# Even and odd features instead of lower and upper halves: a stationary tile of TensorE that takes every second fp32 of a row

## The chip, the core and the metric

The kernel runs on one core of one Trainium2 chip. The metric is device time in microseconds for one execution of the whole kernel, the median of three runs. TensorE, VectorE, ScalarE and the DMA queues of SyncE all work at the same time; the time is set by whichever chain of them ends last.

## What is computed

Two graph layers over 4096 nodes with 256 features, both with the same 4096 x 4096 adjacency matrix. Cut to what matters:

```python
# layer 0
deg = sum(adj, axis=1) + 1e-5
out = ((adj / deg) @ x) @ W_neigh.T + b_neigh + x @ W_self.T + b_self
x1  = layernorm(x + relu(out))
# layer 1
d   = where(rowsum > 0, rowsum ** -0.5, 0)
out = ((d[:, None] * adj * d[None, :]) @ x1) @ W + b
y   = layernorm(x1 + relu(out))
```

The work is in the two products with the adjacency matrix: 4096 x 4096 times 4096 x 256, in fp32.

## The kernel before

**Precision by three passes.** An fp32 number is split into a rounded part (hi) and a remainder (lo), both in the format fp32r, which TensorE takes in one pass. A product is then the sum of three matmuls: x_hi with a_hi, x_hi with a_lo, x_lo with a_hi (line 674). ScalarE makes hi by a copy (L256), VectorE makes lo by a subtraction (L389).

**Tiling of the main matmuls.** The nodes of the result come in 8 blocks of 512 (`NB`, `IB`). For one block the kernel runs over 16 units (`NU`) of two node tiles each (`UJ` = 2, a tile is 128 nodes). For each unit it takes both feature halves `f` and both tiles `q`, and does the three passes: 2 x 2 x 3 = 12 matmuls a unit at L675. In each of them the stationary operand is a 128 x 128 piece of x (128 nodes on the partitions, 128 features in a row), and the moving operand is 128 x 512 of the transposed adjacency matrix. The result, 128 features x 512 nodes, is summed in PSUM in `ps_main[parity][:, f, :]`. The stationary operand changes with every matmul, so each matmul has a weight load of its own (LDWEIGHTS, the rows marked PEld).

**Where the stationary operand lies.** In layer 0 it is read from `xs`, shaped [128, 32, 2, 256]: per partition and node tile, 256 fp32 of hi and then 256 fp32 of lo. In layer 1 it is read from `zs` (28 tiles) and `xs` (4 tiles) in the same layout. The function `stationary` (L154 to L159) gives the slice: 128 neighbouring fp32, from `f * P` on. The first two units of the first block are an exception (L657): they run before hi and lo exist, in plain fp32 straight from the loaded `x_stage(0)` and `raw`. A plain fp32 matmul is done as two passes, so the trace has 16 of them, and there are 24 fewer at L675.

**What surrounds them.** SyncE loads one unit of the adjacency matrix (512 KB) into a ring of four slots (`raw`). ScalarE makes `hi` of it, VectorE `lo`; in layer 0 VectorE also adds the unit into `acc` (L565) for the row sums. TensorE waits for `lo` (`l_ready`, L669), does its 12 matmuls and signals `unit_done`. Slots are freed by `unit_done` and `l_ready`. The order is written out by hand: between units of the main matmuls stand pieces of the previous block's epilogue and of the current block's prologue. Both use `product` (L608): six matmuls with a moving operand of 256 columns (L613), whose stationary operands are the feature-major results `st_hi` and `st_lo`, 128 nodes in a row. One of these groups follows each of the units 1 to 4 (epilogue) and, in layer 0, 9 to 12 (prologue, one unit later in the first block). In layer 0 there is also one group of eight loads and matmuls for the row sums at L634. The last block has an epilogue of its own (L693), after everything else.

**The order of features.** The partition `p` of `ps_main[:, f, :]` is a feature. The second product contracts over it, so the rows of the weight matrices (`contraction_rows`, L709) and of the transposed x (`xt`, L717) must be laid out in the same order of features. Both are arranged on the host, ahead of the kernel.

Of the kernel before, what the change touches and what calls it, by code (L numbers as in the profile page):

```python
# [24 lines left out]
F = 256  # L25
P = 128
FH = F // P
JT = N // P
IB = 512
NB = N // IB  # L30
# [13 lines left out]
def build(nc, x_nat, xt_in, adj_in, wn_in, bn_in, ws_in, bs_in, w1_in, b1_in, out):  # L44
# [6 lines left out]
    with ctx:  # L51
        def sb(name, shape, dt=f32):
            return ctx.enter_context(nc.sbuf_tensor(name, shape, dt))
# [6 lines left out]
        xs = sb("xs", [P, JT, 2, F], f32r)  # L60
# [7 lines left out]
        xt = sb("xt_sb", [P, FH, IB])  # L68
# [54 lines left out]
        def slot(u):  # L123
            return u % RING

        def is_last(e):

            return isinstance(e, int) and e == NB - 1
# [8 lines left out]
        def x_stage(c):  # L137

            if c == 0:
                return acc[:, 1, :].rearrange("p (t f) -> p t f", t=XC)  # L140
            return (res, tt)[c % 2][:, :, :]
# [12 lines left out]
        def stationary(layer, part, jt, f):  # L154

            if layer == 0:
                return xs[:, jt, part, f * P:(f + 1) * P]
            src = zs[:, jt] if jt < ZOWN else xs[:, jt - ZOWN]
            return src[:, part, f * P:(f + 1) * P]  # L159

        def layers(eng, one_block, last_epilogue):

# [444 lines left out]
        def _(pe):  # L607
# [9 lines left out]
            def prologue(b, u):  # L617

                t = u - xt_unit(b)
                if 0 <= t < TB:  # L620
                    if t == 0:
                        pe.wait_ge(wl_ready, 2)
                        pe.wait_ge(xtl_ready, b + 1)

                    product(ps_epi[:, t, F:2 * F], slice(t * P, (t + 1) * P), lambda part, k: ws[:, part, k, :])

            def epilogue(layer, e, parity, u):
                n = e + layer * NB
                if u == 0 and layer == 0:

                    pe.wait_ge(acc_folded, e + 1)
                    pe.wait_ge(ones_set, 1)
                    for t in range(TB):
                        last = pe.matmul(ps_epi[:, TB - 1, t:t + 1], acc[:, parity, t * P:(t + 1) * P],  # L634
                                         ones[:, :], start=True, stop=True)
                    last.then_inc(rs_summed, 1)
                if 1 <= u < 1 + TB:
                    t = u - 1
                    if t == 0:
                        pe.wait_ge(stl_ready, n + 1)  # L640
                    if t == TB - 1 and layer == 0:
                        pe.wait_ge(rs_copied, e + 1)

                    product(ps_epi[:, t, 0:F], slice(t * P, (t + 1) * P),
                            lambda part, k: moving_weight(layer, part, k)).then_inc(tile_done, 1)

            def one_block(layer, b, parity, epi):
                g0 = b * NU + layer * NB * NU
                ps = ps_main[parity]
                for u in range(NU):  # L650
                    if epi is None and u < WHOLE:

                        pe.wait_ge(x_first_full[u], 16)
                        pe.wait_ge(raw_full[slot(u)], 16)
                        for f, q in [(f, q) for f in range(FH) for q in range(UJ)]:
                            jt = u * UJ + q
                            last = pe.matmul(ps[:, f, :], x_stage(0)[:, jt, f * P:(f + 1) * P],  # L657
                                             raw[:, slot(u), q * IB:(q + 1) * IB], start=(jt == 0), stop=False)
                        last.then_inc(unit_done, 1)
                        continue  # L660
                    if epi is None and u % 2 == 0:
                        pe.wait_ge(xl_ready, u // 2 + 1)
                    if layer == 1 and epi[0] == 0:
                        pe.wait_ge(z_ready, UJ * (u + 1))
                    if layer == 1 and epi[0] == 1 and u == 0:
                        pe.wait_ge(wl_ready, 3)


                    pe.wait_ge(l_ready, g0 + (u + 1))  # L669
                    ends = layer == 1 and is_last(b) and u == NU - 1  # L670
                    for f, q in [(f, q) for f in range(FH) for q in range(UJ)]:
                        jt = u * UJ + q
                        cols = slice(q * IB, (q + 1) * IB)
                        for i, (part, mov) in enumerate(((0, hi), (0, lo), (1, hi))):
                            last = pe.matmul(ps[:, f, :], stationary(layer, part, jt, f), mov[:, slot(u), cols],  # L675
                                             start=(jt == 0 and i == 0), stop=(jt == JT - 1 and i == 2))
                        if ends and q == UJ - 1:
                            last.then_inc(half_done, 1)
                    if not ends:
                        last.then_inc(unit_done, 1)  # L680
                    if epi is not None:
                        epilogue(*epi, 1 - parity, u)
                    if layer == 0:
                        prologue(b, u)

            def last_epilogue(epi):
                n = 2 * NB - 1
                passes = [(st_hi, 0), (st_hi, 1), (st_lo, 0)]
                for k in range(FH):
                    pe.wait_ge(stl_ready, n + 1 + k)  # L690
                    for t in range(TB):
# [4 lines left out]
                        if k == FH - 1:  # L696
                            last.then_inc(tile_done, 1)

            layers(pe, one_block, last_epilogue)


# [33 lines left out]
```

## Time and profile before

| | us |
|---|---|
| median of three runs | 800.5 |
| lowest and highest | 799.44, 802.32 |
| span of the profiled execution | 800.8 |
| TensorE matmul busy | 782.1 (98%), 3704 instructions |
| TensorE weight load busy | 653.0 (82%), 3704 instructions |
| VectorE busy | 577.4 (72%) |
| ScalarE busy | 386.9 (48%) |

The profile is of one execution. Matmuls are pipelined: the duration of one (about 390 ns for 512 columns) is longer than the distance from its start to the next one's, so how many are done in a time is read from the starts or from long stretches, not from the duration. A weight load is shown on a lane of its own (PEld) and runs beside the matmul ahead of it. The waits of an engine say how long it stood and for whom; the chain that ended last says which stretches add up to the span.

### The profile page before, as it was taken

Reading aid. Unit: us, or ns where it says so; the run is one execution under the profiler, and the core shown is the slowest. Engines: PE = TensorE matmul, PEld = TensorE weight load, DVE = VectorE, ACT = ScalarE, POOL = GpSimd, SP = SyncE. Lnnn points to the kernel's source line nnn. Section 1 sums busy time; section 2 is a strip of 40 time slices with the busy share of each in tenths; the row PEclk is TensorE's granted clock in tenths of the full one; section 3 lists DMA queues with packets and bytes.
Section 4 is the critical chain, followed back from the end, with each engine's and each line's share of the span. In section 5 each row is a group of like instructions: output and inputs, shape, how many; then the busy total and the mean of one; then the engine's idle time right before and its main releaser. Section 6 shows DMA issues by size and latency. Waiting matters only on the chain.

```text
span 800.8 us, 11034 instructions
## 1 busy us (share of the span) xinstructions
PE 782.1 (98%) x3704; PEld 653.0 (82%) x3704; DVE 577.4 (72%) x868; ACT 386.9 (48%) x528; POOL 0.3 (0%) x6
## 2 busy tenths in 40 slices
PE   7899999999999999999999999999999999999995
PEld 4678888888888888888888888888888888888884
DVE  5799989899898998989966554555546455554643
ACT  3463745536446364454554545445444544545451
POOL 0000000000000000000000000000000000000000
PEclk9999999999999999999999999999999999999998
DMA  8767574755647556465565575746575574657540
GB/s 258 274 252 239 179 244 154 253 183 166 236 155 236 193 174 236 157 233 189 181 227 165 175 255 174 250 162 237 180 236 187 171 246 162 236 180 239 180 158 27
DMA packets 54459, 160.93 MB, mean 201 GB/s; under 512 B 5024, under 2 KB 18464, under 8 KB 54432
## 3 DMA queue, kind: packets, MB, share of 16 engines
q1 hardware_dynamic: 46224, 152.46, 56.6%
q10 hardware_dynamic: 8208, 8.13, 2.9%
q8 instruction: 15, 0.25, 0.1%
q14 instruction: 12, 0.10, 0.0%
HBM read 152.17 MB, written 8.39 MB: 201 GB/s over the span
## 4 chain that ended last, share of the span: by engine, by line
PE 94%; DMA 2%; DVE 2%; ACT 1%; issue 0%; SPq 0%
PE ps_main L675 84%; PE ps_epi L613 8%; DMA raw<-adj_t 2%; PE ps_main L657 1%; PE ps_epi L634 1%; DMA tt<-x_nat 1%; DVE lo L389 0%; DVE acc L565 0%; ACT hi L256 0%; PE ps_epi L693 0%; DVE tt L436 0%; DVE stats L585 0%; DVE tt L419 0%; DVE xs L389 0%; ACT tt L359 0%
## 5 line engine op out<-in xcount | busy, mean ns | idle before, releaser
L256 ACT ACTIVATE hi<-raw 128x1024 fp32r<-128x1024 f32 x254 | 269.4, 1061 | 352.8 <-PE ps_main L675 327.8
L389 DVE TENSOR_TENSOR lo<-raw,hi 128x1024 fp32r<-128x1024 f32 x254 | 310.4, 1222 | 145.3 <-ACT hi L256 145.2
L675 PE MATMUL ps_main<-hi,xs 128*128 128x512 f32 x1136 | 366.3, 392 | 4.3 <-DVE lo L389 4.3
L675 PE MATMUL ps_main<-hi,zs 128*128 128x512 f32 x896 | 283.0, 390 | 0.0
L675 PEld LDWEIGHTS ps_main<-hi,xs 128*128 128x128 f32 x1136 | 214.2, 189 | 49.3 <-DVE lo L389 3.6
L675 PE MATMUL ps_main<-lo,xs 128*128 128x512 f32 x568 | 222.4, 392 | 0.0
L675 PEld LDWEIGHTS ps_main<-hi,zs 128*128 128x128 f32 x896 | 168.3, 188 | 34.3
L675 PE MATMUL ps_main<-lo,zs 128*128 128x512 f32 x448 | 174.7, 390 | 0.0
L565 DVE TENSOR_TENSOR acc<-acc,raw 128x1024 f32<-128x1024 f32 x112 | 136.3, 1217 | 0.0
L675 PEld LDWEIGHTS ps_main<-lo,xs 128*128 128x128 f32 x568 | 107.3, 189 | 20.0 <-issue 0.2
L675 PEld LDWEIGHTS ps_main<-lo,zs 128*128 128x128 f32 x448 | 84.2, 188 | 16.3
L419 DVE SCALAR_TENSOR_TENSOR tt<-ps_epi,d_cur,bias 128x256 f32<-128x256 f32 x32 | 15.4, 483 | 39.2 <-PE ps_epi L613 38.5
L389 DVE TENSOR_TENSOR st_lo<-ps_main,st_hi 128x1024 fp32r<-128x1024 f32 (+1 forms) x17 | 19.8, 1162 | 21.6 <-ACT st_hi L256 21.6
L281 ACT ACTIVATE tt<-tt,nmr,inv_root 128x256 f32<-128x256 f32 x60 | 32.5, 588 | 4.3 <-DVE nmr L473 4.3
L256 ACT ACTIVATE st_hi<-ps_main 128x1024 fp32r<-128x1024 f32 (+1 forms) x17 | 16.6, 978 | 33.3 <-PE ps_main L675 33.3
L275 ACT ACTIVATE ps_epi<-tt,nmean 128x256 f32<-128x256 f32 x60 | 27.5, 459 | 0.0
L436 DVE SCALAR_TENSOR_TENSOR tt<-tt,res 128x256 f32<-128x256 f32 x64 | 26.8, 419 | 0.2
L613 PE MATMUL ps_epi<-ws_sb,st_hi 128*128 128x256 f32 x128 | 24.2, 282 | 0.0
L613 PE MATMUL ps_epi<-wn_sb,st_hi 128*128 128x256 f32 x128 | 24.2, 282 | 0.0
L613 PEld LDWEIGHTS ps_epi<-ws_sb,st_hi 128*128 128x128 f32 x128 | 22.0, 190 | 2.5
L613 PEld LDWEIGHTS ps_epi<-wn_sb,st_hi 128*128 128x128 f32 x128 | 22.0, 190 | 2.5
L613 PE MATMUL ps_epi<-xs,st_hi 128*128 128x256 f32 x112 | 21.2, 282 | 0.0
(74 smaller groups left out, 322.7 us busy)
## 6 DMA issues: line engine op xcount, KB each, us to landing
raw<-adj_t SPq DMA_DIRECT2D x256, 512.0 KB, 3.3
res<-x_nat SPq DMA_DIRECT2D x11, 512.0 KB, 6.4
xt_sb<-xt SPq DMA_DIRECT2D x8, 512.0 KB, 5.0
x_scratch<-tt ACTq DMA_DIRECT2D x8, 512.0 KB, 6.2
res<-x_scratch SPq DMA_DIRECT2D x8, 512.0 KB, 6.0
out<-tt ACTq DMA_DIRECT2D x7, 512.0 KB, 6.4
tt<-x_nat SPq DMA_DIRECT2D x4, 512.0 KB, 6.4
acc<-x_nat SPq DMA_DIRECT2D x2, 256.0 KB, 3.6
```

Of the source, the lines that this page charges most:

```text
L256: return act.activation(dst, src, ACT.Copy)
L275: act.activation(ps_epi[:, t, 0:F], tt[:, t, :], ACT.Square, bias=nmean[:, t:t + 1], accum_out=squares[:, t:t + 1]).then_inc(squares_ready, 1)
L281: act.activation(tt[:, t, :], tt[:, t, :], ACT.Identity, bias=nmr[:, t:t + 1], scale=rstd[:, t:t + 1]).then_inc(x1_ready, 1)
L389: return dve.tensor_tensor(dst, src, hi_part.bitcast(f32), ALU.subtract)
L419: ins = dve.scalar_tensor_tensor(out=tt[:, t, :], in0=ps_epi[:, t, 0:F], scalar=(rdeg, d_cur)[layer][:, t:t + 1], in1=(bias0, bias1)[layer ...
L436: link(dve.scalar_tensor_tensor(out=tt[:, t, :], in0=tt[:, t, :], scalar=0.0, in1=res[:, t, :], op0=ALU.max, op1=ALU.add, accum_out=sums[: ...
L565: dve.tensor_tensor(a, a, raw[:, slot(u), :], ALU.add).then_inc(acc_done, 1)
L613: last = pe.matmul(ps, st[:, k, rows], weight(part, k), start=(k == 0 and q == 0), stop=(k == FH - 1 and q == 2))
L634: last = pe.matmul(ps_epi[:, TB - 1, t:t + 1], acc[:, parity, t * P:(t + 1) * P], ones[:, :], start=True, stop=True)
L657: last = pe.matmul(ps[:, f, :], x_stage(0)[:, jt, f * P:(f + 1) * P], raw[:, slot(u), q * IB:(q + 1) * IB], start=(jt == 0), stop=False)
L675: last = pe.matmul(ps[:, f, :], stationary(layer, part, jt, f), mov[:, slot(u), cols], start=(jt == 0 and i == 0), stop=(jt == JT - 1 and ...
```

## The change

The two feature halves are no longer features 0 to 127 and 128 to 255, but the even and the odd ones. Half `f` takes `f:F:FH`, with `FH` = 2: 128 fp32 at a distance of 8 bytes, over 1020 bytes of the row, where before it took 128 neighbouring fp32, 512 bytes. Partition `p` of `ps_main[:, f, :]` is then feature `2p + f` instead of `f * 128 + p`, and the host lays out the rows of the weights and of the transposed x accordingly. The arrays have the same shapes and sizes as before, and their transfers are the same.

```diff
         def stationary(layer, part, jt, f):
             if layer == 0:
-                return xs[:, jt, part, f * P:(f + 1) * P]
+                return xs[:, jt, part, f:F:FH]
             src = zs[:, jt] if jt < ZOWN else xs[:, jt - ZOWN]
-            return src[:, part, f * P:(f + 1) * P]
+            return src[:, part, f:F:FH]
...
-                            last = pe.matmul(ps[:, f, :], x_stage(0)[:, jt, f * P:(f + 1) * P],
+                            last = pe.matmul(ps[:, f, :], x_stage(0)[:, jt, f:F:FH],
                                              raw[:, slot(u), q * IB:(q + 1) * IB], start=(jt == 0), stop=False)
...
     def contraction_rows(w):
-        return np.ascontiguousarray(w.reshape(FH, P, F).transpose(1, 0, 2))
+        return np.ascontiguousarray(w.reshape(P, FH, F))
...
-        "xt": np.ascontiguousarray(x.T.reshape(FH, P, NB, IB).transpose(2, 1, 0, 3)),
+        "xt": np.ascontiguousarray(x.T.reshape(P, FH, NB, IB).transpose(2, 0, 1, 3)),
```

No instruction is added, removed or moved on any engine. The loads for L613, L634 and L693 read what they read before, without a stride.

## Rows read from the trace of the kernel before

**Rows 1.** All cores: span in us and mean granted TensorE clock.
```profile
core 0: 800.8 us, clock 0.995
```

**Rows 2.** Page: busy time and instructions; shares of the chain that ended last.
```profile
PE 782.1 (98%) x3704; PEld 653.0 (82%) x3704; DVE 577.4 (72%) x868; ACT 386.9 (48%) x528; POOL 0.3 (0%) x6
...
PE 94%; DMA 2%; DVE 2%; ACT 1%; issue 0%; SPq 0%
```

**Rows 3.** Waits on TensorE: who for whom, us in total, times, longest.
```profile
PE ps_main L657 <- DMA raw<-adj_t: 5.4, 1, 5.4
PE ps_main L675 <- DVE lo L389: 4.3, 3, 3.1
```

**Rows 4.** Chain that ended last, in order of time: start us, us, what.
```profile
131.02 13.63 PE ps_main L675 x60
144.65 0.71 PE ps_epi L613 x6
145.36 2.75 PE ps_main L675 x12
...
166.65 0.79 PE ps_epi L634 x8
...
433.38 35.39 PE ps_main L675 x156
468.77 0.71 PE ps_epi L613 x6
```

**Rows 5.** TensorE's groups by form: line, engine, operation, count | busy us, mean ns | idle.
```profile
L675 PE MATMUL ps_main<-hi,xs 128*128 128x512 f32 x1136 | 366.3, 392 | 4.3 <-DVE lo L389 4.3
L675 PE MATMUL ps_main<-hi,zs 128*128 128x512 f32 x896 | 283.0, 390 | 0.0
L675 PE MATMUL ps_main<-lo,xs 128*128 128x512 f32 x568 | 222.4, 392 | 0.0
L675 PE MATMUL ps_main<-lo,zs 128*128 128x512 f32 x448 | 174.7, 390 | 0.0
...
L675 PEld LDWEIGHTS ps_main<-hi,zs 128*128 128x128 f32 x896 | 168.3, 188 | 34.3
```

**Rows 6.** Timeline, 432 to 434 us, TensorE and its loads: start us, us, what.
```profile
432.28 0.39 PE L675 MATMUL ps_main<-hi,zs 128*128 128x512 f32 x1
432.28 0.41 PEld L613 LDWEIGHTS ps_epi<-wn_sb,st_hi 128*128 128x128 f32 x2
432.51 0.40 PE L613 MATMUL ps_epi<-wn_sb,st_hi 128*128 128x256 f32 x2
432.63 0.19 PEld L613 LDWEIGHTS ps_epi<-wn_sb,st_lo 128*128 128x128 f32 x1
432.74 0.28 PE L613 MATMUL ps_epi<-wn_sb,st_lo 128*128 128x256 f32 x1
...
433.10 0.28 PE L613 MATMUL ps_epi<-wn_sb,st_lo 128*128 128x256 f32 x1
433.10 0.19 PEld L675 LDWEIGHTS ps_main<-hi,zs 128*128 128x128 f32 x1
433.22 0.40 PE L675 MATMUL ps_main<-hi,zs 128*128 128x512 f32 x1
433.22 0.19 PEld L675 LDWEIGHTS ps_main<-lo,zs 128*128 128x128 f32 x1
433.45 0.40 PE L675 MATMUL ps_main<-lo,zs 128*128 128x512 f32 x1
```

**Rows 7.** Timeline, 64 to 72 us, loads alone: the eight loads of L634.
```profile
65.48 1.08 PEld L634 LDWEIGHTS ps_epi<-ones,acc 128*128 128x128 f32 x8
```

**Rows 8.** Timeline, 23 to 33 us, where the granted clock was at half.
```profile
28.96 1.05 PE L675 MATMUL ps_main<-hi,xs 128*128 128x512 f32 x2
29.39 0.33 PEld L675 LDWEIGHTS ps_main<-lo,xs 128*128 128x128 f32 x1
29.82 0.63 PE L675 MATMUL ps_main<-lo,xs 128*128 128x512 f32 x1
```

**Rows 9.** Groups of VectorE from 131 to 381 us: busy us, mean ns | idle.
```profile
L389 DVE TENSOR_TENSOR lo<-raw,hi 128x1024 fp32r<-128x1024 f32 x80 | 97.7, 1221 | 19.5 <-ACT hi L256 19.5
```

**Rows 10.** Groups of all engines from 23.5 to 26.5 us, where TensorE stood.
```profile
L389 DVE TENSOR_TENSOR lo<-raw,hi 128x1024 fp32r<-128x1024 f32 x1 | 1.2, 1224 | 6.2 <-ACT hi L256 6.2
```

**Rows 11.** Busy us by stretch, one in each layer: PE, PEld, DVE, ACT.
```profile
200.00:300.00 100.00, 100.00 (x494) 84.72 (x493) 91.68 (x136) 51.19 (x72) 0.00 (x0) 1.00 0.59 199
600.00:700.00 100.00, 100.00 (x465) 83.63 (x464) 53.36 (x81) 47.95 (x64) 0.00 (x0) 1.00 0.61 202
```

## The prediction, made before the changed kernel had run

> **What bounds the kernel now.** I read the span and the granted clock first: one core, 800.8 us, clock 0.995 [rows 1], so nothing is to be explained by the clock but a short stretch near the start. Then the page: the matmul lane is busy 98% of the span, and 94% of the chain that ended last is TensorE [rows 2]. A busy matmul lane proves little, since matmuls overlap, so I looked at the waits: TensorE stood 5.4 us for the first adjacency tile and 4.3 us, in three pieces, for `lo` [rows 3], and for nothing else. From there to the last epilogue the reader is to see an unbroken row of matmuls whose distance sets the time.
>
> That distance comes from the chain in order of time: 60 matmuls of L675 took 13.63 us in layer 0, 227.2 ns each; 156 took 35.39 us in layer 1, 226.9 ns each [rows 4]. The counts by form add up to 1136 + 896 + 568 + 448 = 3048 matmuls at L675 [rows 5]; at 227 ns these are 692 us of the 800.8. The six matmuls of a `product`, 256 columns each, took 0.71 us, 118 ns each [rows 4]. By the counts of the page there are 3704 - 3048 = 656 others: 16 at L657, 64 at L634 (8 groups of 8), 24 at L693, and so 552 at L613, 92 groups of 6.
>
> So one nanosecond more between two main matmuls costs 3.0 us, 0.4% of the kernel. The question of this change is whether a weight load that reads every second fp32 makes that distance longer.
>
> **What the change does, part by part.** It adds, removes and moves no instruction. The transfers of weights and `xt` have the same sizes and land in the same places; the order of features is undone by the host's layout of the contraction rows. Splits, sums and norms read and write whole rows as before. All of this costs nothing, on the path or off it. What is left is the 3048 loads at L675 and the 16 at L657.
>
> First term, **the cover of a load**. The timeline shows when a load starts: the one for the matmul at 433.45 us starts at 433.22, with the matmul ahead of it [rows 6]. It therefore has the whole distance, 227 ns, before its own matmul is due. Its duration in the profile is 188 to 190 ns [rows 5], but that is from start to end with the way through the engine; the time for which it keeps the next one from starting is shorter. In a `product` a load starts at 432.63, its matmul at 432.74, 0.11 us later and before the load's record ends at 432.82 [rows 6]. Loads and matmuls follow each other there every 118 ns. The tightest test of the load alone is L634, whose moving operand is one column: eight loads in 1.08 us, the last one 0.19 long, so (1.08 - 0.19) / 7 = 127 ns from one to the next [rows 7]. So a load of 128 neighbouring fp32 takes its port for 118 ns at most beside fp32r matmuls, and 127 ns at most at L634. Of the 227 ns, 100 to 109 are free. A strided load costs nothing inside a unit as long as it takes less than 227 ns, 1.8 to 1.9 times as long as now.
>
> Second term, **how long a strided load takes**. No row shows one, so I bound it. Low end: it delivers as many numbers, one after the other, and takes what it takes now. An end below that would need the load to be held up by its neighbouring addresses, for which no row speaks; that is the fourth rival. High end: it reads at half the rate, since it covers 1020 bytes where it covered 512; that doubles 118 to 236, or 127 to 254 ns. The nearest row for how fast TensorE can go over addresses is its own moving operand: 512 fp32, 2048 bytes a partition, every 227 ns [rows 4], 9.0 bytes a ns. At that rate the 1020 bytes of a strided load, skipped ones included, take 113 ns, less than the 118 that are there already. That is read on another operand, so it is an analogy and not a proof, but it is the only row in which this engine's reads are seen at work, and it puts the strided load at its present length. I take zero for this term, and keep 0 and 254 - 227 = 27 ns times 3048 = 82 us as its ends.
>
> The Trainium skill (SBUF, Door 1: The DMA port swizzle, the remark on cachelines) says that an SBUF line has 16 bytes, that two hits on a line give full bandwidth, and that each crossing to a new line costs something. With 8 bytes between numbers there are two hits a line, which by the first half of the rule is free; but crossings double from one in four numbers to one in two, which by the second half speaks against the change. The sum would be 800.5 us by the first half and one of the slower rivals by the second.
>
> Third term, **loads with little cover**. A main load behind a matmul of 256 columns has 118 ns and not 227: the load at 433.10 belongs to the matmul at 433.22 [rows 6]. There are 92 of these, one behind each group of L613, and 8 more behind L634: 100. If the load keeps its length, they cost 0. If it took 227 ns, they would cost 100 x 109 ns = 11 us, though nothing inside the units would show. The three stalls before L675 [rows 3] would add the longer load too, under half a us together.
>
> Fourth term, **the other engines**. VectorE is busy 91.68 of 100 us in layer 0, 53.36 in layer 1 [rows 11]. If denser reads of TensorE slowed it by 9%, it would become the bound of layer 0. But the same subtraction takes 1221 ns on average beside full matmuls [rows 9] and 1224 ns in the stretch in which TensorE stood [rows 10]: it does not feel TensorE's reads at all. I take 0. The 16 fp32 loads at L657 also come to nothing: their matmuls are two passes of 512 columns, longer than any main one.
>
> Sum: 800.8 + 0 + 0 + 0 = 800.8 us for an execution like the profiled one, which lies 0.3 above the median of the three runs; on the median this is **800.5 us**, no change.
>
> **Rivals.**
> A, *longer load, hidden inside the units* (slower, slightly). The load grows by a part, to between 130 and 227 ns; only the 100 loads with short cover pay. Price 100 x (12 to 109 ns) = 1 to 11 us: 802 to 812 us. For it: the load's free time is large. Against it: the comparison with the moving operand.
>
> B, *the load becomes the bound* (slower). At half the rate it takes 236 to 254 ns. The distance follows it from 227 ns on, which is where this rival decides: 3048 x (9 to 27 ns) = 27 to 82 us, and 100 x (118 to 127 ns) = 12 to 13 us at the short covers. Time 840 to 896 us. For it: twice the addresses for the same numbers. Against it: the rate of the moving operand. The Trainium skill (TensorE: Matmul & The Clock Gate, LDWEIGHTS (loading the stationary operand)) gives P / 1.2 ns, an estimate of 107 ns here, which twice over is 213 ns; by that figure even half the rate would be rival A. The rows agree with 107 ns so far as they put the load at 118 or less.
>
> C, *the load's reads disturb the moving stream* (slower). At 2.4 GHz, 512 columns are 213.3 ns, and the distance is 227: 13.7 ns more. With 256 columns it is 118 against 106.7: 11.6 ns more. So there is a cost for each load and not for each column. With the clock at half (1.2 GHz) it is gone: two matmuls start from 28.96 on and the next at 29.82, 0.43 us apart each, and 512 columns are 0.427 [rows 8]. That would fit reads of the load that get in the way of a moving stream at full speed, and if it went with the addresses covered it would double: 3048 x 13.7 ns = 42 us, 842 us. Against it: the rows don't say whether the 13.7 ns come from the load's reads or from the mere change of the operand, which an address pattern would leave as it is.
>
> D, *the spread helps* (faster). If the same 13.7 ns came from load and moving stream meeting in one place of the memory, wider spacing could make it smaller; half of it is 21 us, 780 us. Nothing in the trace speaks for it.
>
> That the change doesn't do what it says (the compiled load reads neighbouring numbers after all) would give 800.5 us and is part of the forecast.
>
> **Chances.** Forecast, within 0.3% (2.4 us, about what a measurement of this kernel can tell from no change): 0.74. A 0.06, B 0.08, C 0.07, together slower 0.21. D 0.05. The range begins at 798.0, 0.3% below the forecast, and ends at 813.0, above the highest of A; it holds 0.74 + 0.06 = 0.80 and leaves out B, C and D. The likeliest case alone is 798 to 803 us.
>
> **What would show each step right or wrong.** Right: 156 matmuls of L675 in layer 1 still take 35.4 us, a `product` 0.71 us and the next main matmul starts 0.12 us after its last, main loads still have a mean of 188 ns, and the subtraction on VectorE stays at 1.22 us. A shows as main loads that last longer than 190 ns, with 227 ns between matmuls inside a unit but more behind each L613. B shows as longer loads and a distance that is the load's. C shows as loads of the same 188 ns with a distance of some 240 ns. The prediction is wrong if the distance moves by more than 0.8 ns in either direction.

## The result, and the profile after

The changed kernel takes 817.33 us (median of 4 runs, 816.25 to 819.18), the one before 801.32 us beside it: 1.0209 times as long, 95% interval 1.0193 to 1.0224. That is slower by 2.1%, and outside the range of the prediction. Of the four executions of one kernel below (ring slots offset, strided loads), one took 1174.11 us at a mean granted clock of 0.634, and the other three are compared.

The chain that ended last shows where the time went (start us, us, what); these lines answer to [rows 4].

```profile
129.90 14.00 PE ps_main L675 x60
143.89 0.71 PE ps_epi L613 x6
144.60 2.80 PE ps_main L675 x12
...
438.14 36.40 PE ps_main L675 x156
474.53 0.71 PE ps_epi L613 x6
...
723.90 36.40 PE ps_main L675 x156
```

156 main matmuls now take 36.40 us where they took 35.39: 233.3 ns each instead of 226.9, 6.4 ns more. 12 of them between two groups of L613 take 2.80 us where they took 2.75. A `product` is unchanged at 0.71 us. A whole block in layer 1 went from 46.48 us (six blocks from 433.38 to 712.26 in the trace of before) to 47.63 us (438.14 to 723.90), in layer 0 from 50.39 to 51.37 us. Seven blocks of layer 0 and eight of layer 1 make 7 x 0.98 + 8 x 1.15 = 16.1 us, about the whole difference of the medians (16.0 us); the first block of layer 0, with its waits, is left out of this sum. The spans of the two profiled executions differ less, 800.8 and 814.4 us, because the one of before had a worse start: 9.7 us of stalls on TensorE [rows 3] where this one had 8.0, and some 3 us at half the clock [rows 8], where this one had the whole clock.

The weight loads and the waits on TensorE in the changed kernel, to be read beside [rows 5] and [rows 3] (loads: busy us, mean ns | idle):

```profile
L675 PEld LDWEIGHTS ps_main<-hi,zs 128*128 128x128 f32 x896 | 173.3, 193 | 34.3
...
L613 PEld LDWEIGHTS ps_epi<-wn_sb,st_hi 128*128 128x128 f32 x128 | 21.9, 188 | 2.7
```
```profile
PE ps_main L657 <- DMA raw<-adj_t: 5.0, 1, 5.0
PE ps_main L675 <- DVE lo L389: 3.0, 4, 1.8
```

The strided loads last 193 ns instead of 188; the unstrided ones of L613 last 188 ns, where they took 190 before. TensorE stands no longer than before for anything. VectorE's subtraction is where it was, answering to [rows 9]:

```profile
L389 DVE TENSOR_TENSOR lo<-raw,hi 128x1024 fp32r<-128x1024 f32 x79 | 96.4, 1221 | 22.5 <-ACT hi L256 22.5
```

So a load that is 5 ns longer, with some 100 ns of cover, came with 6.4 ns more between matmuls, and it is the same 233.3 ns in layer 0 as in layer 1, although VectorE has far more to do in layer 0 (92 of 100 us against 53 in the trace of before [rows 11]), which speaks against traffic of VectorE as the cause. That is the riddle which the runs had to solve. They are compared below by the long stretch of layer 1, 156 matmuls at L675 without anything between. (In kernels with one line more in the listing the same lines are L676.)

### The profile page after: what moved, and what is told of

The parts are those of the page before. It is cut to its first block, busy times and chain, and to the rows that moved or that the text cites. A ratio compares the mean times of both kernels' runs of the same rounds, so it can differ in the third digit from the quotient of the medians.

```text
span 814.4 us, 11034 instructions
## 1 busy us (share of the span) xinstructions
PE 797.4 (98%) x3704; PEld 668.5 (82%) x3704; DVE 577.8 (71%) x868; ACT 386.7 (47%) x528; POOL 0.3 (0%) x6
## 4 chain that ended last, share of the span: by engine, by line
PE 96%; DVE 2%; DMA 1%; ACT 0%; issue 0%; SPq 0%
PE ps_main L675 85%; PE ps_epi L613 8%; DMA raw<-adj_t 1%; PE ps_main L657 1%; PE ps_epi L634 1%; DVE lo L389 1%; DVE acc L565 0%; DVE xs L389 0%; PE ps_epi L693 0%; DVE tt L436 0%; DVE stats L585 0%; DVE tt L419 0%; ACT tt L359 0%; ACT hi L256 0%; DVE ws_sb L389 0%
## 5 line engine op out<-in xcount | busy, mean ns | idle before, releaser
L675 PE MATMUL ps_main<-hi,xs 128*128 128x512 f32 x1136 | 371.1, 396 | 3.1 <-DVE lo L389 3.0
L675 PE MATMUL ps_main<-hi,zs 128*128 128x512 f32 x896 | 287.8, 394 | 0.0
L675 PEld LDWEIGHTS ps_main<-hi,xs 128*128 128x128 f32 x1136 | 220.0, 194 | 47.4 <-DVE lo L389 3.0
L675 PE MATMUL ps_main<-lo,xs 128*128 128x512 f32 x568 | 224.1, 395 | 0.0
L675 PEld LDWEIGHTS ps_main<-hi,zs 128*128 128x128 f32 x896 | 173.3, 193 | 34.3
L675 PE MATMUL ps_main<-lo,zs 128*128 128x512 f32 x448 | 176.7, 394 | 0.0
L675 PEld LDWEIGHTS ps_main<-lo,xs 128*128 128x128 f32 x568 | 110.1, 194 | 19.9 <-issue 0.2
L675 PEld LDWEIGHTS ps_main<-lo,zs 128*128 128x128 f32 x448 | 86.7, 194 | 16.6
L613 PE MATMUL ps_epi<-wn_sb,st_hi 128*128 128x256 f32 x128 | 24.2, 281 | 0.0
L613 PE MATMUL ps_epi<-ws_sb,st_hi 128*128 128x256 f32 x128 | 24.1, 280 | 0.0
L613 PEld LDWEIGHTS ps_epi<-wn_sb,st_hi 128*128 128x128 f32 x128 | 21.9, 188 | 2.7
L613 PEld LDWEIGHTS ps_epi<-ws_sb,st_hi 128*128 128x128 f32 x128 | 21.8, 188 | 2.7
L613 PE MATMUL ps_epi<-xs,st_hi 128*128 128x256 f32 x112 | 21.1, 280 | 0.0
```

What stands on the lines that cost most here:

```text
L613: last = pe.matmul(ps, st[:, k, rows], weight(part, k), start=(k == 0 and q == 0), stop=(k == FH - 1 and q == 2))
```

## The experiments

### Is it the loads at all?

The stride is taken back in layer 1 only:

```diff
-            return src[:, part, f:F:FH]
+            return src[:, part, f * P:(f + 1) * P]
...
-        "w1": contraction_rows(as_np(L1_gnn_W)),
+        "w1": np.ascontiguousarray(as_np(L1_gnn_W).reshape(FH, P, F).transpose(1, 0, 2)),
```

> The stride of 8 bytes is kept in layer 0 and taken back in layer 1 (with the host's layout of the last weights). If the added time belongs to each strided load, layer 0 keeps some 233 ns between its main matmuls, layer 1 returns to 227 ns, and the kernel is slower than before by about half of what the whole change costs: 1512 strided loads at L675 times 6.4 ns = 9.7 us, 810 to 811 us. If the order of features or anything outside the loads made the difference, the layers don't part this way.

Measured: 807.4 us, ratio 1.0082 (1.007 to 1.0094). Chain of this kernel:

```profile
387.08 14.00 PE ps_main L675 x60
438.19 35.39 PE ps_main L675 x156
```

Layer 0 keeps 233.3 ns, layer 1 is back at 226.9 to the last digit. The cost sits in the matmuls whose loads are strided, and in nothing else that the change touches. The sum by seven blocks of 0.98 us is 6.9 us, and 6.2 were measured (807.4 against 801.18); my 9.7 had taken each of the 1512 matmuls at 6.4 ns, but the first few behind each group of L613 were slow before too (2.75 us for twelve is 229 ns).

### Is it the number of 16-byte pieces, or the length of the load?

Other distances between the numbers of a load, each in a kernel of its own (the line for layer 1 is shown, the one for layer 0 is changed alike):

```diff
-            return src[:, part, f * P:(f + 1) * P]
+            return src.rearrange("p a f -> p (a f)")[:, 32 * part + f:32 * part + f + 3 * P:3]   # 12 bytes
+            return src.rearrange("p a f -> p (a f)")[:, 2 * part + f:2 * F:4]                    # 16 bytes
+            return src[:, part, f * P:f * P + 1].to_broadcast([P, P])                            # 0 bytes
```

> Every main load takes 128 fp32 at a distance of 12 bytes (from the hi and lo parts together, so the values are not the right ones). By theory L, a cost for each 16-byte piece of memory touched (32 pieces at 4 bytes distance, 64 at 8 bytes, +6.4 ns), this touches 96 pieces: 227 + 2 x 6.4 = 240 ns between main matmuls, about +39 us. By theory S, a fixed price for any distance other than the next number: 233 ns as with 8 bytes, +17 us. By theory B, a load that becomes the bound once the pieces are too many: far more than 240 ns.

> Every main load takes 128 fp32 at a distance of 16 bytes (hi and lo mixed, values not the right ones). Each number lies in a 16-byte piece of its own: 128 pieces. Theory L: 227 + 3 x 6.4 = 246 ns between main matmuls, about +58 us, 859 us. Theory S: 233 ns, 817 us. Theory B, one number a piece stops the load: much above 246 ns, over 900 us.

> Every main load takes the same fp32 128 times (one address; the values are not the right ones). Theory L: 1 piece in place of 32, so 227 - 6.2 = 221 ns between main matmuls, about -19 us, 782 us. Theory S: the price of any distance other than the next number, 233 ns, 817 us. A price only for skipped numbers: 227 ns, 800 us.

| distance | load lasts | between main matmuls | time | ratio |
|---|---|---|---|---|
| 4 bytes (before) | 188 ns | 226.9 ns | | |
| 8 bytes (changed) | 193 ns | 233.3 ns | 817.33 | 1.0209 |
| 12 bytes | 251 ns | 233.7 ns | 822.46 | 1.0268 (1.0253 to 1.0283) |
| 16 bytes | 310 ns | 235.7 ns | 833.8 | 1.0406 (1.0391 to 1.0422) |
| 0 bytes | 187 ns | 228.8 ns | 805.19 | 1.0055 (1.004 to 1.007) |

The rows behind it: of the kernel with 12 bytes its loads by form and its chain, and then the same two of the kernel with 16 bytes.

```profile
L675 PEld LDWEIGHTS ps_main<-hi,zs 128*128 128x128 f32 x896 | 216.2, 251 | 0.0
```
```profile
442.69 36.45 PE ps_main L675 x156
479.15 0.70 PE ps_epi L613 x6
479.85 2.85 PE ps_main L675 x12
```
```profile
L675 PEld LDWEIGHTS ps_main<-hi,zs 128*128 128x128 f32 x896 | 247.2, 310 | 0.0
```
```profile
449.85 36.77 PE ps_main L675 x156
```

Theory L (a price for each piece) falls: 96 and 128 pieces should have given 240 and 246 ns, and a single address 221. The length of the load isn't it either: with 12 bytes the load is 58 ns longer than in the changed kernel and the distance grows by 0.4 ns. With 16 bytes the load itself may have become the bound, as in rival B. Its record is 122 ns longer than with neighbouring fp32; added to the 111 ns from load to load that are measured further down, this gives an estimate of 233 ns, about the whole distance. So the step from 233.7 to 235.7 ns says nothing of how the two streams meet. What the longer load does cost is what the prediction's third term and rival A said: behind a group of L613 twelve matmuls take 2.85 us instead of 2.80, some 0.05 us for each of 100 places, 5 us, and 822.46 - 817.33 is 5.1. Theory S (a fixed price for any stride) fits 8 and 12 bytes, but not 0, where nothing is skipped and the distance is 228.8 ns, 2 ns over before.

Worth keeping from this table is the load itself: every second fp32 costs it 5 ns, every third 63, every fourth 122.

### Does the moving stream have a part in it?

The loads stay as in the kernel before, or as in the changed one; the moving operand becomes one column, 512 times:

```diff
-                            last = pe.matmul(ps[:, f, :], stationary(layer, part, jt, f), mov[:, slot(u), cols],
+                            last = pe.matmul(ps[:, f, :], stationary(layer, part, jt, f),
+                                             mov[:, slot(u), q * IB:q * IB + 1].to_broadcast([P, IB]),
```

> Loads as before (neighbouring fp32), but each main matmul takes the same column of the adjacency tile 512 times, so its moving stream reads one address (the values are not the right ones). Theory M, the load's reads and the moving stream's reads get in each other's way: the distance between main matmuls falls from 227 towards the 213 ns that 512 columns take at 2.4 GHz, some 216 ns, 770 us. Theory I, the 13.7 ns belong to the load or the change of operand alone: still 227 ns, 800 us.

> The same with the loads of the changed kernel (every second fp32). Theory M: no difference from the run with neighbouring fp32, both near 216 ns. Theory I: 233 ns, so 6.4 ns above the run with neighbouring fp32, whatever the moving stream reads.

One run each: 764.97 and 764.87 us, against 800.23 for the kernel before beside them. Chain and loads by form, first with neighbouring fp32 (two fences), then with every second:

```profile
678.15 33.67 PE ps_main L675 x156
```
```profile
L675 PEld LDWEIGHTS ps_main<-hi,zs 128*128 128x128 f32 x896 | 169.3, 189 | 23.1
```
```profile
678.13 33.67 PE ps_main L675 x156
```
```profile
L675 PEld LDWEIGHTS ps_main<-hi,zs 128*128 128x128 f32 x896 | 174.8, 195 | 17.9
```

This decides between M and I. The strided load still lasts 6 ns longer, yet the distance is 215.8 ns in both, and the whole cost of the stride is gone: it needs the moving stream's own reads beside it. Gone too are 11 of the 13.7 ns by which the kernel before was over the 213.3 ns of 512 columns (800.23 - 764.97 = 35 us), and 17.5 ns in the changed kernel. That the reads of the weight load and those of the moving stream hold each other up is shown for the 6.4 ns by which the two kernels differ. For the 11 ns below it is likely but not shown: no run has the full moving stream without a load beside it, so a part may be the moving stream's alone. The load that read one address (0 bytes) left the distance at 228.8 ns.

The Trainium skill (TensorE: Matmul & The Clock Gate, Step-by-step: what each phase is for) says that the two have separate read ports and that a load takes no read bandwidth from a running matmul. With fp32r the pattern of a load that is fully hidden moved the distance by 6.4 ns, and only while the moving stream read its own addresses, so the trace doesn't agree, and the measurement decides.

### What the load costs by itself

Each main matmul is split into four of 128 columns with a load each:

```diff
+                            for c in range(4):
+                                last = pe.matmul(ps[:, f, c * P:(c + 1) * P], stationary(layer, part, jt, f),
+                                                 mov[:, slot(u), q * IB + c * P:q * IB + (c + 1) * P],
...
```

> Each main matmul of 512 columns is split into four of 128, each with a load of its own of the same neighbouring fp32. 128 columns take 53 ns at 2.4 GHz, so the load sets the distance. By the groups of 256 columns, at most 118 ns, the load's own time with neighbouring fp32 is 107 to 118 ns: 12192 x 107 to 118 ns = 1305 to 1439 us for the main matmuls, 1410 to 1550 us in all.

> The same split with every second fp32. If a strided load takes its port longer by the 6 ns by which its record is longer, the distance grows by 6 ns and the kernel by 12192 x 6 ns = 73 us over the split with neighbouring fp32. If the load takes no longer by itself and only meets the moving stream differently, the difference is under 20 us. If the load read at half the rate, 12192 x 107 ns = 1300 us more.

Timelines of both while the clock was whole, neighbouring fp32 first:

```profile
30.10 0.97 PEld L676 LDWEIGHTS ps_main<-hi,xs 128*128 128x128 f32 x8
```
```profile
30.48 1.02 PEld L676 LDWEIGHTS ps_main<-hi,xs 128*128 128x128 f32 x8
```

Less the last load's 0.19 and 0.20 us, seven distances are 0.78 and 0.82 us: 111 and 117 ns from load to load. The load takes 6 ns longer, as its record says, and not twice as long; the expected 107 to 118 ns were right. The expected totals (1410 to 1550 us) were not: 2686.54 and 2688.95 us, because after the first slices the granted clock went to half and stayed there, although the page shows the matmul lane full (tenths in 40 slices, 67 us each):

```profile
PE   9999999999999999999999999999999999999998
...
PEclk9755555555555555555555555555555555555555
```

At half the clock the two kernels are alike within 0.1%, so these totals say nothing of the stride.

### Is it the stride, or where the two streams begin?

The work is that of the kernel before; the addresses of `hi` and `lo` move, and with them those of all tensors allocated behind them (`acc`, `st_hi` and others), but not `xs`, `zs` and `raw`. First each ring slot begins 16 bytes further off than the last:

```diff
-        hi = sb("hi", [P, RING, UW], f32r)
-        lo = sb("lo", [P, RING, UW], f32r)
+        hi = sb("hi", [P, RING, UW + 4], f32r)[:, :, 0:UW]
+        lo = sb("lo", [P, RING, UW + 4], f32r)[:, :, 0:UW]
```

> Loads of neighbouring fp32. The rows of hi and lo get 16 bytes more, so that the four ring slots begin 0, 16, 32 and 48 bytes off; the work is the same. If load and moving stream meet because both begin at a multiple of 512 bytes, some slots show less than 227 ns between main matmuls, down to 216 at best, and the kernel gains up to 3/4 of 33 us. If the offset plays no part, all slots stay at 227 ns and the time at 800 us.

> The changed kernel (every second fp32 in the loads) with the slots of hi and lo 0, 16, 32 and 48 bytes off. If the 6.4 ns come from how the two streams fall on each other in the memory, the slots differ and some fall below 233 ns; if they go with the strided load as such, all slots stay at 233 ns and the time at 817 us.

Measured: 812.46 us, ratio 1.0129 (1.0104 to 1.0154), with neighbouring fp32, and 814.85 us, ratio 1.0156 (1.0124 to 1.0187), with the strided loads. With 32 bytes a slot the tensors no longer fit into SBUF, the memory of the partitions, so that offset has no time. The first was expected to be faster or unchanged and is slower: moving the operands by a few bytes costs most of what the stride cost, with loads of 188 ns.

```profile
722.96 36.13 PE ps_main L675 x156
```
```profile
723.56 36.24 PE ps_main L675 x156
```

231.6 against 232.3 ns. Here the stride costs 0.7 ns, not 6.4, and the strided loads come 1 ns below the 233.3 ns of the changed kernel. So I shifted all slots alike, by one small tensor ahead of `hi`:

```diff
+        shim = sb("shim", [P, 4])      # 16 bytes; 8 and 16 and 24 of them make 32, 64 and 96 bytes
         hi = sb("hi", [P, RING, UW], f32r)
```

> Loads of neighbouring fp32; hi and lo both begin 16 bytes later in memory, all slots alike. If the start address of the moving operand within a few 16-byte pieces decides how the streams meet, the distance leaves 227 ns (231 to 233, 810 to 817 us). If only the changing offsets from slot to slot did it, 227 ns and 801 us.

> The same with 32 bytes. If the meeting repeats every 32 bytes, 227 ns and 801 us whatever the shift by 16 shows; otherwise another distance between 216 and 241 ns.

> The same with 64 bytes. If the meeting repeats every 64 bytes, 227 ns and 801 us.

> The changed kernel with hi and lo both 16 bytes later. If the 6.4 ns go with the strided load, 233 ns and 817 us as without the shift. If they go with the meeting of start addresses, another distance than 233 ns, and the same as with neighbouring fp32 and this shift, within 2 ns.

> Every second fp32 in the loads, hi and lo begin 64 bytes later. If strided loads find no cheap meeting at any start, 233 ns and 817 us as at shifts of 0 and 16. If start addresses decide for them as for the others, 229 ns and 805 us as with neighbouring fp32 at this shift.

> Loads of neighbouring fp32, hi and lo begin 96 bytes later. By the shifts of 16 and 32 (233.3 ns) and of 64 (228.9), a repeat every 64 bytes gives 233 ns and 817 us; anything under 227 ns would be a faster kernel than before.

And once with the same tensor ahead of `xs`, so that stationary and moving operands both begin 16 bytes later:

> Loads of neighbouring fp32; stationary operands (xs, zs) and moving operands (hi, lo) all begin 16 bytes later in memory. If the place of the two relative to each other decides, 227 ns between main matmuls and 801 us as in the kernel before. If the moving operand's own address decides, 233 ns and 817 us as with the shift of hi and lo alone.

| | neighbouring fp32 | every second fp32 |
|---|---|---|
| as they were | 226.9 ns | 233.3 ns, 1.0209 |
| `hi`, `lo` + 16 bytes | 233.3 ns, 1.0213 (1.0192 to 1.0234) | 233.4 ns, 1.0241 (1.0224 to 1.0258) |
| + 32 bytes | 233.3 ns, 1.021 (1.0193 to 1.0227) | |
| + 64 bytes | 229.0 ns, 1.0054 (1.0037 to 1.0071) | 233.3 ns, 1.0201 (1.0172 to 1.0231) |
| + 96 bytes | 233.3 ns, 1.0201 (1.0175 to 1.0228) | |
| both operands + 16 bytes | 226.9 ns, 0.9993 (0.998 to 1.0005) | |

The chain of four of these: neighbouring fp32 shifted by 16 bytes (a stretch in each layer), by 64 bytes, both operands shifted, and every second fp32 shifted by 64:

```profile
131.11 14.00 PE ps_main L676 x60
...
725.38 36.40 PE ps_main L676 x156
```
```profile
433.44 35.73 PE ps_main L676 x156
```
```profile
710.89 35.39 PE ps_main L676 x156
```
```profile
724.43 36.39 PE ps_main L676 x156
```

The loads of the kernel shifted by 16 bytes are as short as before:

```profile
L676 PEld LDWEIGHTS ps_main<-hi,zs 128*128 128x128 f32 x896 | 168.0, 187 | 39.5
```

This settles most of it. 233.3 ns is what a main matmul costs at three of the four shifts tried with neighbouring fp32. The 226.9 ns of the kernel before are a cheap meeting of the two streams, and they come back when both operands are shifted together by 16 bytes: their place relative to each other decides, not the address of the moving operand. The shift of `hi` and `lo` also moved them against `raw`, from which ScalarE and VectorE make them. That this traffic does it is spoken against by layer 0 and layer 1, where VectorE is busy 90% and 52% of the time in the kernel shifted by 16 bytes (us 200 to 300, 600 to 700): the distance is 233.3 ns in both. Where VectorE and ScalarE both stand still for three matmuls in a row (ten places in the trace), it is 233.4 ns. A strided load doesn't find such a meeting at any of the shifts of all slots tried with it (0, 16 and 64), not at 0 and 64, where neighbouring fp32 does. What the change took away is this cheap meeting, not the speed of the load. Where neighbouring fp32 have lost it too, the stride as such costs 0.1 ns a matmul (all shifted by 16 bytes) or 0.7 ns (slot by slot); why a strided load finds none stays open.

### A stride in the moving operand

```diff
-                        cols = slice(q * IB, (q + 1) * IB)
+                        cols = slice(q, UW, UJ)
```

> Loads of neighbouring fp32, and the moving operand of each main matmul takes every second fp32 of the unit's 1024 (the nodes come out in another order, so the values are not the right ones). If the two streams get in each other's way by the number of 16-byte pieces that they touch together, the 128 more pieces of the moving stream cost more than the 32 of the strided load did: above 233 ns, over 817 us. If only the load's own pattern counts, 227 ns, 800 us.

Measured: 1477.96 us, ratio 1.8433 (1.839 to 1.8476). Chain and loads by form:

```profile
1314.20 70.38 PE ps_main L675 x156
```
```profile
L675 PEld LDWEIGHTS ps_main<-hi,zs 128*128 128x128 f32 x896 | 186.1, 208 | 209.3 <-issue 208.6
```

451 ns a matmul where it was 227; the granted clock was 0.989 on average and 1.00 in this stretch. The loads of neighbouring fp32 beside this stream last 208 ns instead of 188, which fits two streams that disturb each other. Both theories had a direction here, neither the size: the moving operand at a distance of 8 bytes is read at about half the rate (512 columns in 427 ns would be exactly half). The stationary operand with the same stride lost 5%.

## Why the prediction was wrong

**The cover of a load**: right as far as it went. The load's own 111 ns lie within the bound of 118, and with 12 bytes a load whose record is 251 ns (an estimate of 174 ns from load to load, 111 + 63) costs nothing inside a unit by its length. But the sentence "a strided load costs nothing inside a unit as long as it takes less than 227 ns" was the step that failed. It took the cover for the only way in which a load can reach the path. In its place the runs showed a cost of 6.4 ns a matmul at a load only 5 to 6 ns longer, gone when the moving stream read one address, and there without any stride when `hi` and `lo` began 16 bytes later. A load that is hidden in time still meets the reads of the stream that it hides beside.

**How long a strided load takes**: taken as 0 more, measured as 6 ns more; a small miss that cost nothing by itself. That it came so near was luck, for its argument was wrong. I set the load beside the moving operand's 9.0 bytes a ns, skipped bytes included. The moving operand can't do that: strided by 8 bytes it takes twice as long. The row that I called the only one at work was of a stream read without gaps, and said nothing about gaps.

**The Trainium skill's cachelines** (SBUF, Door 1: The DMA port swizzle): for the load alone the first half of the rule nearly held, two numbers a line at 8 bytes cost 5% (193 ns for 188) and one a line at 16 bytes cost 122 ns on top of 188. For the moving operand it did not hold: two hits a line gave half the rate, 451 ns for 227. And what decided the time here, how the two streams fall on each other, isn't in the rule at all.

**Loads with little cover**: right, and seen in the kernel with 12 bytes, 5 us for 58 ns more a load. In the changed kernel the 5 ns are too few to show.

**The other engines**: right, 1221 ns on VectorE before and after.

**Rival C** was the mechanism, with 0.07 of the chance, and it was mis-sized. It took the 13.7 ns for a price that goes with the addresses covered, and doubled it: 42 us. Of the 13.7 ns, 11 go when the moving stream reads one address; the stride raised them to 17.5, and not in proportion to the addresses, but because the streams no longer fall on each other as they did. I had the evidence for weighing it higher: the 13.7 ns a load at the whole clock and nothing at half, which I set out and then put aside because the rows didn't say whose they were. (Its second point was weaker than it looked: the 118 ns of a 256-column matmul are little more than the 111 ns of a load alone, so there the load may set the distance, and they don't show a cost for each load.) An unexplained 6% in the very quantity that the change touches, multiplied by 3048, should have been given more than 0.07, and the range should have reached 20 us up.

**The count of what it costs** was nearly right: 3 us for each ns gives 19.5 us for 6.4 ns, and 16.0 came, because the first matmuls behind each group had already paid a part before. One slip stands in the sum: it set the span of the profiled execution, 800.8, beside a median of whole times, 800.5. A whole time is some 1.8 us longer than its span (816.25 and 814.4 in the changed kernel), so that execution was about 2 us above the median and not 0.3. The forecast rests on the median and is not touched by it.

What stays open: why a shift of 64 bytes is nearly as cheap as none and 16, 32 and 96 are not, how much of the 11 ns is owed to the loads at all, and whether another shift comes nearer to the 215.8 ns of a moving stream that reads one address. No faster kernel with the right result was found; at best 35 us lie there.

## What to carry to other kernels

A matmul stream that runs at the clock's pace but 5% over it is worth a look: here weight loads, fully hidden in time, held up the moving operand, and how much depended on where the two began in memory relative to each other (226.9 to 233.3 ns). So before a changed access pattern is blamed or praised, shift the operands by 16 bytes without it, since a kernel may owe 2% to the layout it happens to have. Keep the moving operand without gaps: every second fp32 cost this kernel 84%. In the stationary operand every second fp32 cost 2.1%, every third 2.7%, every fourth 4.1%.

## What had not been expected of the hardware

- With all ring slots placed alike and loads of no more than 8 bytes distance, main matmuls of 512 columns take one of a few distances on average and stay there for whole blocks: 226.9, 228.8 to 229.0 or 233.3 ns, by pattern and start address; 215.8 ns with a moving operand of one address.
- A shift of `hi` and `lo` by 16 bytes made the kernel slower by 2.1%, the shift of both operands by 16 bytes changed nothing.
- The same stride of 8 bytes costs 5% on the stationary operand (111 to 117 ns from load to load) and doubles the time of the moving one (227 to 451 ns).
- With a load for each 128 columns the matmul lane is busy 99% of the span, and the granted clock still falls to half after some 100 us and stays there.
